# Input blocks three and four get their own time-step series, with their cumulative sums in the fifth and ninth step

## What is computed

```
dt = jax.nn.softplus(hidden_states @ Win.T + dt_bias)
A = -jnp.exp(A_log_bias)
g = dt * A
...
G = jnp.cumsum(gc, axis=-1)
decay = jnp.where(causal, jnp.exp(G[..., :, None] - G[..., None, :]), 0.0)
y_intra = jnp.einsum('bhnij,bhnjd->bhnid', scores * decay, xc)
```

## Time and profile before

| | us |
|---|---|
| median of 3 runs | 1636.06 (1635.18 to 1636.61) |
| the profiled execution, its own time | 1634.31 |
| its span, first to last instruction | 1632.5 |
| mean granted TensorE clock | 0.990 of full speed |
| busy: PE, POOL, DVE, ACT | 97%, 87%, 84%, 67% of the span |

### The profile page before, as it was taken

How to read it: one execution, slowest core, us unless ns; L and a number is a source line. 1 busy time by engine, 2 the same in 40 slices (tenths; PEclk the granted TensorE clock), 3 DMA queues, 4 the chain that set the end, 5 groups by cost and what they waited for, 6 DMA issues and landing times.

```text
span 1632.5 us, 33589 instructions
## 1 busy us (share of the span) xinstructions
PE 1587.2 (97%) x11028; PEld 885.4 (54%) x11028; DVE 1368.7 (84%) x2945; ACT 1093.5 (67%) x2987; POOL 1412.8 (87%) x1316
## 2 busy tenths in 40 slices
PE   7898999999999999999999999999999999999986
PEld 6554555555555555555555555555555555555554
DVE  7988788888879888797879888887888878788976
ACT  5666676676766667766766667666676767676653
POOL 5777899888988999888988999888998989888964
PEclk8999999999999999999999999999999999999998
DMA  6022233232343224231532223222332224222222
GB/s 223 28 56 67 59 74 85 65 73 53 79 85 78 53 59 107 50 85 46 92 83 62 63 66 87 72 72 53 86 84 59 72 46 105 65 65 58 48 46 104
DMA packets 208012, 118.76 MB, mean 73 GB/s; under 512 B 173792, under 2 KB 174816, under 8 KB 206816
## 3 DMA queue, kind: packets, MB, share of 16 engines
q1 hardware_dynamic: 207840, 116.63, 30.0%
HBM read 70.19 MB, written 4.46 MB: 46 GB/s over the span
## 4 chain that ended last, share of the span: by engine, by line
PE 74%; POOL 13%; DVE 7%; issue 4%; ACT 2%; ACTq 0%; POOLq 0%; DVEq 0%
PE B L323 24%; PE B L325 23%; PE B L324 23%; POOL ROWS L1428 2%; POOL QS L1415 2%; POOL RR L1461 2%; POOL PL L1450 1%; POOL WVL L1446 1%; DVE WL L1701 1%; POOL ZS L1454 1%; POOL RM L1458 1%; POOL WVF L1438 1%; POOL K L1422 1%; PE B L553 1%; DVE PF L1645 1%
## 5 line engine op out<-in xcount | busy, mean ns | idle before, releaser
L323 PE MATMUL B<-WH,XTH 128*128 128x128 bf16 (+1 forms) x992 | 270.0, 297 | 5.0 <-DVE VL L1630 4.3
L324 PE MATMUL B<-WL,XTH 128*128 128x128 bf16 (+1 forms) x992 | 269.8, 297 | 0.0
L325 PE MATMUL B<-WH,XTL 128*128 128x128 bf16 (+1 forms) x992 | 269.8, 297 | 0.0
L1415 POOL TENSOR_TENSOR QS<-QS,SIN 128x512 f32<-128x512 f32 x160 | 219.5, 1372 | 33.6 <-ACT QS L1142 33.0
L323 PE MATMUL B<-XTH,WH 128*128 128x512 bf16 x640 | 243.3, 380 | 1.1 <-DVE G L1635 1.1
L325 PE MATMUL B<-XTH,WL 128*128 128x512 bf16 x640 | 243.3, 380 | 0.0
L324 PE MATMUL B<-XTL,WH 128*128 128x512 bf16 x640 | 243.1, 380 | 0.0
L1694 DVE SCALAR_TENSOR_TENSOR YF<-B,RR,G 128x128 f32<-128x128 f32 x512 | 144.1, 344 | 113.4 <-POOL RR L1461 113.3
L1174 ACT ACTIVATE PF<-ROWS,NG 128x128 f32<-128x128 f32 x512 | 162.8, 390 | 79.3 <-POOL ROWS L1428 78.9
L1454 POOL TENSOR_TENSOR ZS<-YF,ZS 128x512 bf16<-128x512 f32 x128 | 158.0, 1235 | 64.4 <-ACT ZS L1212 64.2
L1428 POOL TENSOR_TENSOR ROWS<-ROWS,AFTER 128x512 f32<-128x512 f32 x128 | 190.1, 1485 | 2.5 <-DMA ROWS<-rows_dram 2.5
(11 more groups left out here) (209 smaller groups left out, 4319.8 us busy)
## 6 DMA issues: line engine op xcount, KB each, us to landing
ROWS<-rows_dram SPq DMA_DIRECT2D x128, 256.0 KB, 3.2
STAGE<-in_wall SPq DMA_DIRECT2D x108, 256.0 KB, 2.8
ACC<-in_x SPq DMA_DIRECT2D x3, 1024.0 KB, 9.1
out<-ACC SPq DMA_DIRECT2D x3, 1024.0 KB, 3.9
ZT<-ZS SPq DMA_TRANSPOSE x128, 3.1
ACC<-in_x SPq DMA_DIRECT2D x4, 256.0 KB, 3.7
COS<-in_cos SPq DMA_DIRECT2D x1, 1024.0 KB, 12.8
SIN<-in_sin SPq DMA_DIRECT2D x1, 1024.0 KB, 14.8
```

The source lines that it names most:

```text
L323: nc.tensor.matmul(out_, ah, bh, start=first, stop=False)
L324: nc.tensor.matmul(out_, ah, bl, start=False, stop=False)
L325: return nc.tensor.matmul(out_, al, bh, start=False, stop=last)
L1415: nc.gpsimd.tensor_tensor(QS[:, sl, :], QS[:, sl, :], SIN[:, t0:t0 + TB], ALU.mult).then_inc(sin_ready.sem, 1)
```

## The change

It makes three units of the two pairs. Unit 0 is blocks 0 and 1 as before. Unit 1 is block 2 alone and unit 2 block 3 alone, each on tiles of 128x128. `|x|` and the exponential of unit 1 move to the end of step 0, those of unit 2 to the end of step 4. Part 0 of unit 1 is at the end of step 1, part 1 at the end of step 2, parts 2 and 3 at the end of step 3; for unit 2 the steps are 5, 6 and 7. The sums of block 3 move from step 6 to step 8 and their sending from step 7 to step 9.

```
-SUMS_STEP = {4: 2, 6: 3}
-SEND_STEP = {5: 2, 7: 3}
+SUMS_STEP = {4: 2, 8: 3}
+SEND_STEP = {5: 2, 9: 3}
+ABS_STEP = {0: 1, 4: 2}
+SERIES_STEP = {1: (1, 0), 2: (1, 1), 3: (1, 2), 5: (2, 0), 6: (2, 1), 7: (2, 2)}
...
-        def pair(T, q):
-            return T[:, 2 * q * BH:2 * (q + 1) * BH]
+        def blocks_of(q):
+
+            return range(2) if q == 0 else range(q + 1, q + 2)
+
+        def unit(T, q):
+            return T[:, blocks_of(q)[0] * BH:(blocks_of(q)[-1] + 1) * BH]
...
         def pe_sums(pe, f):
 
-            pe.wait_ge(d_g.sem, d_g.at(f // 2, 0))
+            pe.wait_ge(d_g.sem, d_g.at(max(0, f - 1), 0))
...
             hi(0, 0, 4)
-            act_dt_exp(act, 1)
             gate(0, 0, 2, 8)
...
                 if s == 1 and now:
                     slot("C")
+                if g == 0 and n in ABS_STEP:
+                    act_dt_exp(act, ABS_STEP[n])
...
             q_lo(0, 0, 1)
-            dve_dt_abs(dve, 1)
             q_lo(0, 0, 2)
-            dve_series(dve, 1, 0)
             decayed(0, 0)
...
-                if g == 0 and n == 0:
-                    dve_series(dve, 1, 1)
...
-                if g == 0 and n in (1, 2):
-                    dve_series(dve, 1, n + 1)
+                if g == 0 and n in ABS_STEP:
+                    dve_dt_abs(dve, ABS_STEP[n])
+                if g == 0 and n in SERIES_STEP:
+                    dve_series(dve, *SERIES_STEP[n])
+                    if SERIES_STEP[n][1] == 2:
+                        dve_series(dve, SERIES_STEP[n][0], 3)
```

More of the change, by code:

```diff
@@ L766, in dve_dt_abs @@
         def dve_dt_abs(dve, q):
-            dve.wait_ge(d_in.sem, d_in.at(2 * q + 1, 0))
-            nc.vector.scalar_tensor_tensor(pair(EG, q), pair(DT, q), -1.0, pair(DT, q), ALU.mult, ALU.max).then_inc(d_abs.sem, 1)
+            dve.wait_ge(d_in.sem, d_in.at(blocks_of(q)[-1], 0))
+            nc.vector.scalar_tensor_tensor(unit(EG, q), unit(DT, q), -1.0, unit(DT, q), ALU.mult, ALU.max).then_inc(d_abs.sem, 1)
         def act_dt_exp(act, q):
             act.wait_ge(d_abs.sem, d_abs.at(q, 0))
-            nc.scalar.activation(pair(EG, q), pair(EG, q), ACT.Exp, scale=-1.0).then_inc(d_e.sem, 1)
+            nc.scalar.activation(unit(EG, q), unit(EG, q), ACT.Exp, scale=-1.0).then_inc(d_e.sem, 1)
         def dve_series(dve, q, part):
-            X, E, R, S, Y = (pair(T, q) for T in (DT, EG, WJ, DCH, NG))
+            X, E, R, S, Y = (unit(T, q) for T in (DT, EG, WJ, DCH, NG))
             if part == 0:
@@ L800, in dve_series @@
             dve.wait_ge(a_ready.sem, 1)
-            nc.vector.scalar_tensor_tensor(rows(Y), rows(X), -1.0, by_head(ALOG), ALU.mult, ALU.mult).then_inc(d_g.sem, 1)
+            nc.vector.scalar_tensor_tensor(rows(Y), rows(X), -1.0, by_head(ALOG, BLK * len(blocks_of(q))), ALU.mult, ALU.mult).then_inc(d_g.sem, 1)
         def sums_bank(f):
```

## The result

| | before | after |
|---|---|---|
| median, us | 1635.06 (1633.81 to 1636.61, 6 runs) | 1646.03 (1644.08 to 1655.23, 6 runs) |
| ratio of the two | | 1.0083, interval 1.0065 to 1.0100 |
| the profiled execution, its own time | 1634.31 | 1652.25 |
| its span | 1632.5 | 1650.4 |
| mean granted clock | 0.990 | 0.984 |

By the medians the change makes the kernel 11.0 us slower. The ratio in the table isn't that of the medians: its interval, 0.65 to 1.00%, is 10.6 to 16.4 us, so 11.0 lies at the lower end of it. The six runs after the change are 11 us apart. The forecast was 1647.6 us, in a range of 1638.5 to 1654.0.

What follows compares the result with a forecast made beforehand. DVE, with POOL, was taken to set the pace up to step 4 and PE from step 5. Terms -1.4 + 0 - 0.6 + 4.0 + 1.4 + 0 + 6.7 + 1.4 = +11.5 on 1636.1 gave 1647.6 us, range 1638.5 to 1654.0.

Steps and rivals of the forecast that it cites:

- 1 prologue: Prologue: decayed(0) comes 0.56 us sooner and the clock may stay up in the next fill; -1.4 us, bounds -0.6 and -2.3.
- 1, 2 steps 0 and 1: Steps 0 and 1: taking part 1 out gives nothing, |x| costs nothing, part 0 replaces three instructions; 0 us.
- 3 step 2: End of step 2: four narrow instructions replace four that took 3.1 us; -0.6 us taken, between 1.3 gained and nothing.
- 4 step 3: Step 3, before block 2's sums: seven instructions, some held up by POOL, lengthen PE's wait; +4.0 us, bounds 2.3 and 5.5.
- 4 clock: Behind the wait for block 2's sums: TensorE's clock falls; +1.4 us, bounds 0 to 1.7.
- 6 step 7: Step 7, before block 3's moved sums: DVE 2.5 us late plus seven instructions at 4.0; +6.7 us, bounds +3.2 and +11.1.
- 6 clock: Behind the wait for block 3's moved sums: TensorE's clock falls again; +1.4 us, bounds 0 to 1.7.
- Part 5: Steps 5 and 6: unit 2's parts 0 and 1 make DVE about 2.5 us late by step 7's end; PE unaffected, 0 us.
- POOL hardly disturbs: Rival: narrow instructions pass POOL almost undisturbed, parts 2 and 3 cost 2.3 us each; +3.3 to +6 us, chance 0.15.
- part 7: SP, ACT and POOL: the moved sending, sums' ACT work and WJ product lie beside PE's work; 0 us.
- The sum of all high bounds: Whole kernel: the prediction put the sum of all its terms' high bounds at about +19 us.
- the wait for VL: Step 2: PE's wait for VL stays near 4.3 us, with its slow clock.

Runs made afterwards that it cites:

- the first two experiments: Kernel before with only block 3's sums and sending moved, ratio 0.9988; changed kernel with every part of both narrow series one step earlier, ratio 1.0020.
- The short POOL instructions: Changed kernel with the three POOL instructions beside parts 2 and 3 cut to 4 of their columns; 1640.04 us, ratio 1.0042 to the kernel before.
- with PE kept busy, the busy PE: Changed kernel with 24 unused matmuls of 512 columns before the wait of the sums in steps 4 and 8; 1641.15 us, ratio 1.0049.
- all seven experiments made from it: Changed kernel with series earlier, pair unsplit, series in DVE's gaps, quarter width, short POOL instructions, PE busy, or |x| in prologue; 1637.18 to 1651.40 us.
- the first experiment: Kernel before with only block 3's sums moved to step 8 and their sending to step 9; 1631.93 us, ratio 0.9988.
- the two runs with parts in step 0: Kernel before, block 3's sums in step 8, the pair's part 2, then parts 2 and 3, moved to step 0; 1632.47 and 1631.64 us.
- The last experiment: Changed kernel with |x| and the exponential of unit 1 back in the prologue; 1651.40 us, ratio 1.0113 to the kernel before.
- the three experiments with the same program up to there: Changed kernel with parts 2 and 3 at quarter width, with three short POOL instructions, or with PE kept busy; 1645.14, 1640.04 and 1641.15 us.
- the series a step earlier: Changed kernel with every part of both narrow series one step earlier; 1637.18 us, ratio 1.0020 to the kernel before.

## Why the prediction was right, step by step

Mid's +14.4 us against the predicted +11.5, both traces read at the same events (the number is the prediction's part):

| step | predicted | in the trace | read at |
|---|---|---|---|
| 1 prologue | -1.4 | -0.3 | first KF of step 0, 104.55 and 103.72 |
| 1, 2 steps 0 and 1 | 0 | +0.9 | PF of step 2, 132.14 and 132.24 |
| 3 step 2 | -0.6 | -1.4 | PF of step 3, 144.61 and 143.27 |
| 4 step 3 | +4.0 | +4.7 | sums of block 2, 154.25 and 157.64 |
| 4 clock | +1.4 | +2.8 | PE at the moved sums, 202.1 and 208.29 |
| 6 step 7 | +6.7 | +6.3 | `read_state` of step 8, 202.93 and 215.42 |
| 6 clock | +1.4 | +1.3 | last stage, 1557.98 and 1571.79 |

(The table allows for the 0.55 us by which the prologue of after came earlier, and for the 0.83 us of sums that before has in step 6. The first row on the clock also holds whatever unit 2 cost PE in steps 5 and 6, and the +6.3 holds 0.6 us by which the sums themselves were slower at the low clock.)

*That the number is so close is in part luck.* The terms are off by 0.1 to 1.4 us, four too low and three too high, and mid comes out 2.9 us above their sum. The medians moved 3.4 us less than mid, and the two misses nearly cancel.

*What held.* Both waits were named with their place, their releaser and their size: 6.0 and 5.7 us stand against "5 to 6" and 6.7. The step-7 wait is a little shorter than reckoned since PE also comes late to it. That DVE has no gap between gating and `add_out` shows in the first two experiments from two sides: no wait without the series there, and hardly any with the series elsewhere. The basis for 4.0 us was that a two-input instruction waits for POOL's end: two hits with some overlap were taken, and there were three, 4.73 us. The short POOL instructions show the rest, 2.16 us, against 2.3 that I had as the undisturbed price. Part 5, which had DVE 2.5 us late before step 7, is near as well: with PE kept busy `add_out` of chunk 5 ends 53.95 us behind the sums of block 2, where the pair's series leaves it at 47.15; 4.75 of the 6.80 are the seven instructions, and 2.1 are left.

The rule of the Trainium skill that the prediction weighed (page "SBUF — State Buffer", section "Who interferes with whom"), that an instruction holds the shared ports for its whole length, agrees with 3.84 us beside three POOL instructions of full length against 1.26 beside short ones. The rival "POOL hardly disturbs" falls with the same pair.

*Part 1, the prologue, was mis-sized, and for a reason I hadn't seen.* DVE at the prologue's end, after, in place of the earlier trace rows:

```profile
94.95 1.13 DVE L1652 SCALAR_TENSOR_TENSOR PF<-B,DT,PF 128x128 f32<-128x128 f32 x4 [4.04 <-ACT PF L1180]
```

The series is out of the way and DVE idles for 4 us, but ACT's decay came only 0.4 us sooner (93.56 for 93.95, and the whole prologue 0.55), so what I had put at 0.56 gave 0.3. The larger part of the step was the clock, "may stay up". PE's idle time before the fill stayed at 1.05 us in after, and at 1.04 or 1.05 in the experiments made from it. In the profiled execution of after the clock fell and the fill took 4.29 us; in all seven experiments made from it it took 2.60 or 2.61, and in four of these the program is the same up to there. In the first experiment it took 2.60 where the same program had taken 4.29 in before. So the edit alone doesn't decide this fall. But it may make it rarer: with the pair's part 0 in the prologue 3 of 4 traces have the long fill (before and the two runs with parts in step 0), without it 1 of 8. Twelve traces don't settle that. The term was right to have bounds 1.7 us apart, and the profiled pair fell on the side on which it gives nothing.

*Steps 0 and 1 (parts 1, 2 and 7) were put at zero and cost 0.9.* Part 0 in step 1 took 2.62 us, where the instructions that it replaced took 2.92 of DVE's queue. But |x|, which I had at 0.3 us "beside POOL's unbroken work", took 0.76, and the exponential that needs it made ACT wait 3.1 us and POOL 1.1. The last experiment showed that this costs 1.24 us. The prediction had no term for this exponential; its part 7 put ACT and POOL at 0 as lying "beside PE's work", by the duration of what moves and not by what is queued behind its wait.

*Part 3, in step 2, took the favourable end* (1.67 us for the four, 141.60 to 143.27, where the four wide ones took 3.11): one was held up and three were not.

*The clock behind the first wait was undersized.* It was taken at 1.4 us with bounds of 0 and 1.7, from one slow fill in front of step 0. It stayed low for longer (0.50 from 158 to 162 and 0.67 to 164), and the stretch cost 2.8. Together the two cost 4.1 in the table; the busy PE showed 4.3.

*Two slips that change nothing.* The sum of all high bounds is about +20 and not +19. And the wait for VL was to keep its 4.3 us and its low clock: in the profile of after it was 2.5 with the clock at 1.00 behind it, in the three experiments with the same program up to there 4.0.

*What stays open.* Mid says +14.4, the span +17.9, and the medians +11.0. The last stage took 78.6 us in the profiled execution of after, as in the last experiment, and 74.5 in that of before. With the 1.7 us in front of step 0 these 4.1 us make 5.8 of the 6.2 us by which the profiled execution lies above its median. That the other executions of after lacked both is likely and not shown, since they have no trace. In the last experiment all four times are high, so there the slow last stage may be the rule, and why it should be is open. Put together: 17.9 less 4.1 and 1.7 for an execution without these two, less 0.8 since before's profiled execution lies that much under its median, is 11.3 us against the 11.0 measured. This sum fits and isn't a proof.

## What to carry to other kernels

Price an instruction set between others by who runs beside it: with two inputs in SBUF next to a busy POOL it cost up to one POOL instruction here (some 1.2 us for one of 0.29), with little regard to its width, and splitting a tile in two doubles the number of these. A chain whose result nobody needs yet belongs anywhere but between a step's last work and the hand-over for which TensorE waits, and a moved instruction that waits is to be priced by all that is queued behind it. Idle time read from a profile isn't room for a chain until one has looked at what the other engine with the same ports does in it.

## What was not expected of the hardware

- **A one-input instruction is held up too.** The prediction took 0.22 us for these. TENSOR_SCALAR of 128x128 took 0.21 and 0.22 us in two places and 0.77, 0.77, 0.84 and 1.06 us in four others, beside POOL. The first of step 2, after:

```profile
141.60 0.77 DVE L797 TENSOR_SCALAR EG<-NG 128x128 f32<-128x128 f32 x1
142.41 0.94 DVE L800 SCALAR_TENSOR_TENSOR EG<-EG,NG 128x128 f32<-128x128 f32 x3
```

  The same section of the Trainium skill says that `tensor_scalar` can use the shared pair as well, and the rows agree. The reciprocal was never held up (0.95 us both times), nor was PF, which reads PSUM (1.11 to 1.13 us).
- **The clock can stay low behind a wait although PE is busy without a break,** for some 5.7 and 4 us behind two waits of 6.0 and 5.7 us: the sums behind them took 1.65 us instead of 0.94. Behind waits of 1.5 us it stayed at 1.00 (the series a step earlier), and of two waits of 3.0 and 3.3 us it fell behind the shorter one and not behind the longer (POOL's short instructions). In front of step 0 it was low in 4 of 12 traces, behind a wait of 1.04 or 1.05 us that all 12 have. Filling the two long waits with 24 useless matmuls each gave 4.3 us back.
- **The same program meets the low clock in one execution and not in another:** 4.29 or 2.60 us for one fill, 72.4 to 78.6 us for the last stage. The Trainium skill, page "TensorE: Matmul & The Clock Gate", section "Part 1: The HAM clock gate", says that the number of slow matmuls at a kernel's start varies from run to run. The rows here aren't of a start, but they show the like in front of step 0 and at the end. With 1.7 and 4.1 us it is as large as the terms in the table above, so a difference of that size between two single traces has to be looked for in the clock first.
